# Low-rank rows of two row blocks mixed in one step of 256 columns, and the gated rows' low part ahead of the second gating

## The reference

```python
x = x + x @ W0.T + 0.5 * (x @ A0[lab0]) @ B0.T
x = x + x @ w_eff.T                      # quantised weight + low-rank delta
x = x + x @ W2.T + 0.5 * (x @ A2[lab2]) @ B2.T
base = x @ W3.T
logits = x @ Wr.T + 5 * one_hot(lab7)
topw, topi = top_k(logits, 2)
gates = sum(one_hot(topi, 8) * softmax(topw)[..., None], axis=-2)
h = einsum('btd,erd->bter', x, A3)
x = x + base + 2 * einsum('bter,bte,eor->bto', h, gates, B3)
```

## Time and profile before

| | us |
|---|---|
| median of three runs (607.70 to 608.03) | 607.87 |
| the profiled execution, timed | 607.86 |
| its span in the trace | 606.1 |
| TensorE busy, share of the span | 600.0 (99%) |
| TensorE weight loads | 536.4 (89%) |
| VectorE busy | 391.9 (65%) |
| ScalarE busy | 214.4 (35%) |
| GpSimd busy | 79.7 (13%) |

### The profile page before, as it was taken

The page is one execution under the profiler, slowest core; times in us unless marked ns, Lnnn a source line. Parts: engine busy times, 40 slices in busy tenths (PEclk is TensorE's granted clock), DMA queues, the critical chain, the costliest instruction groups (busy, mean ns, idle before and its releaser), DMA issues.

```text
span 606.1 us, 9230 instructions
## 1 busy us (share of the span) xinstructions
PE 600.0 (99%) x3247; PEld 536.4 (89%) x3247; DVE 391.9 (65%) x727; ACT 214.4 (35%) x403; POOL 79.7 (13%) x111
## 2 busy tenths in 40 slices
PE   8999999999999999999999999999999999999998
PEld 7999999899999999888888788788888888888887
DVE  3488998999989829200004598967474747475653
ACT  3434233346233129211111278433333333333330
POOL 2101010023000000000000005040404040303120
PEclk9999999999999999999999999999999999999999
DMA  9963220362000030200001110222131313030301
GB/s 263 263 164 92 100 72 1 43 199 89 1 1 1 1 36 1 45 1 0 0 0 35 40 30 1 50 91 79 60 88 50 96 43 109 30 121 17 101 4 71
DMA packets 57824, 37.69 MB, mean 62 GB/s; under 512 B 26684, under 2 KB 51516, under 8 KB 57796
## 3 DMA queue, kind: packets, MB, share of 16 engines
q1 hardware_dynamic: 57796, 37.31, 22.2%
HBM read 28.91 MB, written 8.39 MB: 62 GB/s over the span
## 4 chain that ended last, share of the span: by engine, by line
PE 90%; DVE 7%; ACT 2%; DMA 1%; issue 0%; POOL 0%; POOLq 0%
PE acc L1414 48%; PE acc L1551 29%; PE acc L1572 4%; PE aux L1401 2%; DVE q L1041 2%; PE acc L1574 2%; DVE qtmp L1040 1%; PE acc L1580 1%; PE acc L1581 1%; PE aux L1489 1%; DVE w_lo L945 1%; DVE hg_lo L952 1%; DMA g<-in_L_cond_W_dram 1%; PE acc L1401 1%; ACT hg_hi L611 1%
## 5 line engine op out<-in xcount | busy, mean ns | idle before, releaser
L1414 PE MATMUL acc<-hg_hi,w_hi 128*128 128x352 f32 (+2 forms) x384 | 87.2, 335 | 1.3 <-DVE w_lo L945 0.9
L1414 PE MATMUL acc<-hg_lo,w_hi 128*128 128x352 f32 (+2 forms) x384 | 85.8, 331 | 0.0
L1414 PE MATMUL acc<-hg_hi,w_lo 128*128 128x352 f32 (+2 forms) x384 | 85.6, 330 | 0.0
L1414 PEld LDWEIGHTS acc<-hg_hi,w_hi 128*128 128x128 f32 x384 | 66.3, 188 | 2.9 <-DVE w_lo L945 1.3
L1414 PEld LDWEIGHTS acc<-hg_hi,w_lo 128*128 128x128 f32 x384 | 67.3, 188 | 0.0
L1414 PEld LDWEIGHTS acc<-hg_lo,w_hi 128*128 128x128 f32 x384 | 67.2, 188 | 0.0
L945 DVE TENSOR_TENSOR w_lo<-a_t,w_hi 128x1024 fp32r<-128x1024 f32 (+2 forms) x9 | 9.9, 1105 | 82.1 <-ACT w_hi L603 82.1
L1041 DVE TENSOR_TENSOR q<-q,qtmp 128x1024 f32<-128x1024 f32 x48 | 59.5, 1240 | 1.7
L768 ACT CAST left_hi<-xr 128x512 fp32r<-128x512 f32 x64 | 39.6, 622 | 51.1 <-PE acc L1551 33.6
L539 POOL TENSOR_TENSOR xr<-xr 128x512 f32<-128x512 f32 x28 | 35.7, 1298 | 130.4 <-DVE left_lo L1190 129.1
L1551 PE MATMUL acc<-rh_a,left_hi 128*128 128x512 f32 (+1 forms) x132 | 52.7, 399 | 0.0
(11 more groups left out here) (213 smaller groups left out, 1042.5 us busy)
## 6 DMA issues: line engine op xcount, KB each, us to landing
x_st<-in_x_dram SPq DMA_DIRECT2D x64, 128.0 KB, 2.9
out_dram<-part SPq DMA_DIRECT2D x31, 256.0 KB, 2.8
g<-in_L_cond_W_dram SPq DMA_DIRECT2D x8, 512.0 KB, 7.2
w_st<-in_L_cond_W_dram SPq DMA_DIRECT2D x8, 512.0 KB, 4.6
a_t<-in_L_cond_weight_dram SPq DMA_DIRECT2D x8, 512.0 KB, 5.0
w_raw<-in_L_cond_weight_dram SPq DMA_DIRECT2D x8, 512.0 KB, 4.3
a_raw<-in_L_cond_lora_A_dram SPq DMA_DIRECT2D x5, 128.0 KB, 3.6
a_raw<-in_L_cond_lora_A_dram SPq DMA_DIRECT2D x20, 32.0 KB, 1.9
```

The costliest lines, as they stand in the source:

```text
L1414: last = pe.matmul(acc[0:a.shape[-1], slot, bank * BANK:bank * BANK + c1 - c0], a[:, k, :], b[:, k, c0:c1], start=(at == 0 and n == 0), st ...
```

## The change

It touches batches 1 to 7 alone; batch 0 keeps its order of work, with only the tiles placed anew (`vt` now has two halves, `vm` is one tile for both blocks).
- `mix` is called once, behind the first k of M4, for both blocks: two matmuls of 256 columns. `m_high` and `m_low` are called once each, over 256 columns. The semaphores `mix_done`, `m_hd`, `m_split` count one a batch in place of two.
- `correct_others(0)` stands behind M4, ahead of `correct_others(1)`.
- `turn_g(0)` moves from behind the third k of M6 to behind the second k of M5. `turn_g(1)` stands behind the second k of M7 in place of the first.
- On VectorE the low part of S1 moves ahead of `m_low` and `best_two(0)`, and `g_low(0)` moves ahead of the low part of S4 and of `gated(1)`.
- On ScalarE `m_high(0)` goes. Transposed gated rows get other places in `aux` (`AUX_GATED`).

```diff
 # ScalarE, pair
                 v_high(0)
                 copy_second(1)
                 left_high(b, "S2")
-                m_high(0)
                 v_high(1)
                 done("M2")
                 left_high(b, "S1")
-                m_high(1)
+                m_high()
...
 # VectorE, pair
-                def m_low(h):
-                    dve.wait_ge(m_hd, b * 2 + (h + 1))
-                    dve.tensor_tensor(vm[h][2 * R:], aux_at(h, 1)[2 * R:], vm[h][2 * R:].bitcast(F32),
-                                      ALU.subtract).then_inc(m_split, 1)
+                def m_low(h=None):
+                    if first:
+                        dve.wait_ge(m_hd, h + 1)
+                        low, mixed = vm[2 * R:, h], aux_at(h, 1)
+                    else:
+                        dve.wait_ge(m_hd, b + 2)
+                        low, mixed = vm[2 * R:].rearrange("p h r -> p (h r)"), AUX_MIX
+                    dve.tensor_tensor(low, mixed[2 * R:], low.bitcast(F32), ALU.subtract).then_inc(m_split, 1)
...
                 left_low(b, "S2")
-                m_low(0)
                 v_low(1)
+                left_low(b, "S1")
+                m_low()
                 best_two(0)
-                m_low(1)
                 gated(0)
-                left_low(b, "S1")
                 best_two(1)
+                g_low(0)
                 left_low(b, "S4")
                 gated(1)
-                g_low(0)
                 if ahead:
                     x_turn(b, 0, 1)
                     sel_low(b + (E_FIRST + 1))
...
 # TensorE, pair
+                def mix(h=None):
+
+                    pe.wait_ge(v_split, h + 1 if first else b * 2 + 2)
                     pe.wait_ge(tsel_ready, b * 2 + 2)
-                    pe.matmul(aux_at(h, 1), tsel_h[:], vt[:], start=True, stop=False, skip_group_check=True)
-                    pe.matmul(aux_at(h, 1), tsel_l[:], vt[:], start=False, stop=True,
-                              skip_group_check=True).then_inc(mix_done, 1)
+                    at, rows = (aux_at(h, 1), vt[:, h]) if first else (AUX_MIX, vt[:].rearrange("p h r -> p (h r)"))
+                    pe.matmul(at, tsel_h[:], rows, start=True, stop=False, skip_group_check=True)
+                    pe.matmul(at, tsel_l[:], rows, start=False, stop=True, skip_group_check=True).then_inc(mix_done, 1)
...
                 wait_out("C11")
                 product("Y", "A12", "B21", range(1), start=True)
-                mix(0)
+                if first:
+                    mix(0)
                 product("Y", "A12", "B21", range(1, 2))
                 turn_v(1)
                 product("Y", "A12", "B21", range(2, HALF)).then_inc(step_done, 1)
-                correct_others(0)
-
                 if first:
+                    correct_others(0)
                     pe.wait_ge(acc_free, 2 + PASSES)
+
                 wait_out("C21")
                 product("W", "A22", "T4", range(1), start=True)
                 mix(1)
                 product("W", "A22", "T4", range(1, HALF)).then_inc(step_done, 1)
+                if not first:
+                    correct_others(0)
                 correct_others(1)
...
                 product("X", "S2", "T2", range(3))
-                turn_g(0)
+                if first:
+                    turn_g(0)
                 product("X", "S2", "T2", range(3, HALF)).then_inc(step_done, 1)

                 wait_left("S1")
                 wait_out("C12")
-                product("Z", "S1", "T1", range(HALF), start=True).then_inc(step_done, 1)
+                product("Z", "S1", "T1", range(2), start=True)
+                if not first:
+                    turn_g(0)
+                product("Z", "S1", "T1", range(2, HALF)).then_inc(step_done, 1)
...
-                product("X", "S3", "T3", range(1))
+                turn_at = 1 if first else 2
+                product("X", "S3", "T3", range(turn_at))
                 turn_g(1)
-                product("X", "S3", "T3", range(1, HALF)).then_inc(step_done, 1)
+                product("X", "S3", "T3", range(turn_at, HALF)).then_inc(step_done, 1)
```

More of the change, by code:

```diff
@@ L223, in build @@
         tsel_h, tsel_l = place("tsel_h", 36864, [P, P], F32R), place("tsel_l", 37376, [P, P], F32R)
-        vm = [place(f"vm{h}", 37888 + 512 * h, [P, P], F32R) for h in range(2)]
+        vm = place("vm", 37888, [P, 2, P], F32R)
         hgt_h = [place(f"hgt_h{h}", 38912 + 512 * h, [P, P], F32R) for h in range(2)]
         hgt_l = [place(f"hgt_l{h}", 39936 + 512 * h, [P, P], F32R) for h in range(2)]
-        v_sb, vt = place("v_sb", 40960, [P, 2, 2 * R]), place("vt", 41472, [P, P], F32R)
+        v_sb, vt = place("v_sb", 40960, [P, 2, 2 * R]), place("vt", 35840, [P, 2, P], F32R)
         hg = place("hg", 32768, [P, E, RE])
@@ L250, in aux_at, with gated_at @@
             return aux[:, h * BANK + n * P:h * BANK + (n + 1) * P]
+        AUX_MIX = aux[:, P:3 * P]
+        AUX_GATED = (aux[:, BANK + 2 * P:BANK + 3 * P], aux[:, 3 * P:4 * P])
+        def gated_at(first, h):
+            return aux_at(h, 2) if first else AUX_GATED[h]
         w3_in = [sem(f"w3_in{k}") for k in range(KT)]
@@ L854, in v_high, with m_high @@
                     act.wait_ge(v_tr, b * 2 + (h + 1))
[L855 to L859, removed]
+                    act.copy(vt[:, h], aux_at(h, 0)).then_inc(v_hd, 1)
+                def m_high(h=None):
+                    if first:
+                        act.wait_ge(mix_done, h + 1)
+                        act.copy(vm[:, h], aux_at(h, 1)).then_inc(m_hd, 1)
+                    else:
+                        act.wait_ge(mix_done, b + 2)
+                        act.copy(vm[:].rearrange("p h r -> p (h r)"), AUX_MIX).then_inc(m_hd, 1)
                 def g_high(h):
                     act.wait_ge(g_tr, b * 2 + (h + 1))
-                    act.copy(hgt_h[h][:], aux_at(h, 2)).then_inc(g_hd, 1)
+                    act.copy(hgt_h[h][:], gated_at(first, h)).then_inc(g_hd, 1)
                 def exponential(h):
@@ L1602, in correct_others @@
                     at = E_BANK[h][:, EH:E_W]
-                    pe.matmul(at, vm[h][:], vb_hi[:, D:C_LOW2], start=False, stop=False, skip_group_check=True)
-                    pe.matmul(at, vm[h][:], vb_lo[:, D:C_LOW2], start=False, stop=True,
+                    pe.matmul(at, vm[:, h], vb_hi[:, D:C_LOW2], start=False, stop=False, skip_group_check=True)
+                    pe.matmul(at, vm[:, h], vb_lo[:, D:C_LOW2], start=False, stop=True,
                               skip_group_check=True).then_inc(r_done, 1)
@@ L1608, in turn_g @@
                     pe.wait_ge(hg_ready, b * 2 + (h + 1))
-                    turn_tile(aux_at(h, 2), hg[:].rearrange("p e r -> p (e r)")).then_inc(g_tr, 1)
+                    turn_tile(gated_at(first, h), hg[:].rearrange("p e r -> p (e r)")).then_inc(g_tr, 1)
                 def wait_left(name):
```

15 lines of the change are left out of this document (7 added, 8 removed).

## The result

The changed kernel takes 614.60 us (median of four runs, 614.02 to 614.92) against 607.79 for the kernel before, measured beside it (607.62 to 608.03). The ratio is 1.0111, with a 95% interval of 1.0093 to 1.0128. The forecast was 615.1, its range 612.3 to 617.2. The profiled execution took 614.02, with a span of 612.3 us, against 607.86 and 606.1.

The account below looks back on a forecast made before the run. TensorE, busy 29.80 of 29.80 us a batch, was taken to bound the kernel. Six batches 1.24 us longer, less 0.22 in the last, add 7.2 us to about 607.86: 615.1, range 612.3 to 617.2.

Parts of the forecast that it names:

- The merged pair: TensorE's mixing: one pair of 256 columns costs 0.26 us against 0.48 for two pairs, saving 0.22 a batch.
- `best_two(0)`: VectorE's step behind the moved correction `correct_others(0)`: starts 2.73 us later in the batch.
- Nothing else in the gap: VectorE ahead of the corrections: S1's low part (0.72) and the wider subtraction (at most 0.64) fit, costed at nothing.
- `g_low(0)`: VectorE's low part behind `turn_g(0)`: starts at 472.76, set by the transpose; `finish("Y")` does not wait, slack 0.42 us.
- First transposes: `x_turn(b, 0, 1)` on VectorE: starts at 475.27 against 473.43, 1.84 us later.
- `g_low(1)`: VectorE's step ahead of `finish("W", 1, 0)`: starts at 478.32, so TensorE waits 1.13 us, on the path in full.
- The second wait: Next batch's first product waits for C22, delayed through the staging tile's DMA: 0.33 us more, with slack 0.60.
- Sum: Batches 1 to 6 each 1.24 us longer, batch 7 0.22 shorter: +7.2 us, giving 615.1.
- one wait alone: Rival: only the wait for `g_low(1)` costs, the one for C22 does not; 613.1 us, chance 18%.
- A `g_low(0)` late for TensorE: Rival: `g_low(0)` slips 0.3 us through ScalarE or chained small operations, 1.8 us more; 617, chance 10%.
- The case of no loss: Rival: VectorE has the new low part in time, so the merger alone counts; 606.3 us, chance 5%.
- the partial wait of 0.3 to 0.7 us: Rival: small steps overlap better in the new order, so TensorE waits less; about 610 us, chance 5%.

Follow-up runs that it names:

- the version without waits: Changed kernel with `mix` behind product Y, corrections behind W's second k, `turn_g(0)` between X and Z, `g_low(1)` and C21 early: 606.1 us, ratio 0.9975.
- C21 early: Changed kernel with C21's addition moved ahead of the second transposes, into VectorE's wait for the DMA: 612.8 us, ratio 1.0085.

## Why the prediction was right
The times of the earlier trace rows are put on one scale here, from `v_copy(0)` of the batch (459.80 before, 461.46 after).

- **The merged pair.** 0.26 was taken. From 466.70 to 467.40 there are 0.70 us, less two regular matmuls 0.25. Saved 0.23 a batch against 0.22; the last batch shortened by 0.20, the version without waits by 0.24. The price from 256-column products of another line held. The isolated figures of the Trainium skill (TensorE: Matmul & The Clock Gate, "Back-to-back issue gap"), by which the merger is worth nothing, are given there for a matmul by itself, and the section says that at small widths they under-count a stream that loads weights too. The trace agrees: the isolated figures do not describe this stream, in which every matmul loads weights of its own: here 128 columns take 0.11 us and 256 take 0.12.
- **`best_two(0)`**: 2.73 later was predicted; it starts 8.16 after `v_copy(0)` where it was 5.38, 2.78 later.
- **Nothing else in the gap.** S1's low part and the 64x256 subtraction (0.43, within 0.32 to 0.64) end at 468.31, VectorE then idles 1.31 us. Costed at nothing, rightly.
- **`g_low(0)`** bound by the transpose: predicted 12.96 after `v_copy(0)`, measured 13.05. `finish("Y")` did not wait.
- **First transposes**: 1.84 later predicted, 1.92 measured (13.63 to 15.55).
- **`g_low(1)`**: predicted 18.52, measured 18.54 (the transposes came 0.08 later than forecast and the way from them to `g_low(1)` is 2.99 in place of 3.05, so two small errors cancel). TensorE's first matmul starts 0.44 behind it (480.00 to 480.44; 0.45 was taken). It would have come at 478.87 + 2 x 0.23 = 479.33: a wait of 1.11, predicted 1.13.
- **The second wait** was there, for the reason given, and is the term that was off. C22 starts at 485.97, and 485.97 + 0.85 = 486.82 is when the first product starts; TensorE was free at 486.14 + 2 x 0.23 = 486.60. That is 0.22, not 0.33. The transfer was at fault: from the first to the second transposes it took 5.97 us in this batch and 5.95 in the mean of the six. I had carried over the 6.22 of the one batch read in the kernel before (6.09 in the mean of its six, 5.91 to 6.29), and the slack of 0.60 that I took for all six makes up for only 0.10 of that.
- **Sum**: 30.99 us a batch against 31.04, times six: 7.15 against 7.44. With -0.20 for the last batch the loop costs +6.95 where +7.2 was predicted; the median moved by 6.8.
- **What the sum did not say.** It added a wait of 1.13 and one of 0.33, as though each could be had back. In the changed kernel both only show a loop that is 1.2 too long, and taking the larger away moved it whole into the smaller. The prediction had the means, since its second wait is worked out as 1.24 less the 0.91 that is there already, but it names the first as on the path in full. The first counts in full only where the longer cycle is shortened: with C21 early a batch is 0.93 above the kernel before.
- **A slip in the range.** 0.3 us a batch either way is 1.8 us, which gives 613.3 to 616.9, not 616.7. Nothing hangs on it.

The rivals: one wait alone (613.1) is out, as both are in the trace; its number came true where C21 is early (612.8). A `g_low(0)` late for TensorE did not occur: `finish("Y")` shows no wait. The case of no loss needed `g_low(1)` 1.13 us earlier, and the partial wait of 0.3 to 0.7 us needed it 0.4 to 0.8 earlier; it came when predicted.

## What to carry to other kernels
When a step that feeds a long fixed queue is moved back to merge it with another, follow that queue to every place at which the bounding engine waits for it, and across the loop's edge: here 0.2 us of saved matmuls a batch brought 1.2 us through a staging tile that is loaded once the queue has read it. Two waits in one loop are first to be tested for being one: take the larger away and see whether the other grows, and see in the trace which stretch the length of a batch follows. And the cheap form of the same merger was to keep the consumer's time and move the producer up, which gave the saving without the delay.

## What the runs showed of the hardware
A short matmul of 128 columns with its own weights takes 0.11 us here and one of 256 columns 0.12, so from 128 to 256 columns the width is nearly free. Refilling the staging tile by four DMAs of 128 KB takes 5.8 to 6.6 us over all runs, from the start of the first transposes to that of the second. In one batch of the changed kernel 1.5 us of it pass until SyncE issues the first DMA (477.01 to 478.50), 1.9 us while it issues the four, and 2.6 us from there to the second transposes. As long as TensorE bounds the loop this scatter is not seen: in the kernel before the batches are 29.76 to 29.88 us long with 5.91 to 6.29 of transfer. In the changed kernel it is in the time: the kernel with `turn_g(0)` earlier had a batch of 31.36 us where the transfer took 6.46.
